# FFN's up product by Wo times W1 folded on the chip, W2's parts kept for two tiles, one gather per tile

## The chip, the cores and the metric

The kernel runs on one core of a Trainium2 chip. The metric is the device time of one execution in microseconds (us), as the median of the runs shown. The engines are TensorE (PE, with its weight loads shown apart as PEld), VectorE (DVE), ScalarE (ACT), GpSimd (POOL) and SyncE (SP, which here only issues DMAs).

## What is computed

The layer takes `x` of 2 x 1024 tokens with 256 channels. A mixture of experts, then attention, then a residual sum give `x2`. What the change touches comes behind that:

```python
def _L0_cond2_ref(x, ...):                 # a state space block, N = 64 states
    ...
    state = decay * state + dt * b_t * u_t # scan over the 1024 tokens
    ys = c_t * state                       # [B, L, 64]
    return y @ Wo + bo                     # Wo is [64, 256]; called x3 below

def _L0_ffn_ref(x3, Wr, br, W1, W2):       # 8 experts, each token uses one
    route = sigmoid(x3 @ Wr + br)
    max_prob, max_ind = max(route), argmax(route)
    out[token] = max_prob * (gelu(x3 @ W1[e]) @ W2[e])   # e = max_ind; W1 256x1024, W2 1024x256
x = x2 + _L0_ffn_ref(_L0_cond2_ref(x2, ...), ...)
```

## The kernel before

All matrix work that has to be precise is done with fp32r operands split in two: `hi` is the operand rounded to fp32r (a copy on ACT), `lo` is what is left (a subtraction on DVE), and a product is three matmuls, hi times hi, hi times lo and lo times hi (`three`, L1676).

The last part of the kernel has two stages. In the **routing stage** the 64 states of every token are in `seq_u` (one batch in each half of the partitions). PE makes the router's logits from them (`make_logits`), and DVE, ACT and PE find the expert of each token, its place among the tokens of that expert, and from that `token_s` (which token stands in which lane of which tile), `prob_s` and `tile_i` (the expert of each tile). Meanwhile PE makes x3 = y Wo + bo for all tokens (`bias_x3`, `make_x3`), ACT copies it out of PSUM (`x3_to_sbuf`) and stores it to the DRAM tensor `x3_d` (`store_x3`); SP has stored x2 to `x2_d`. Between these, `keep_warm` runs matmuls whose result nobody reads.

In the **tile stage** the tokens are worked on in 23 tiles of 128 tokens, each of one expert. For a tile POOL gathers its rows of x3 (`load_x3`) and of x2 (`load_x2`) with an indirect DMA each and scatters the result (a third one, L767). PE turns the tile's x3 (`turn_x`, 2 transposes), makes the up product (`half_up` twice, 12 matmuls of 512 columns: 2 chunks of 128 channels x 2 halves x 3), turns the hidden tile (`turn_h`, 8 transposes) and makes the down product (`expert_down`, 24 matmuls of 256 columns in two halves). ACT does gelu, the hi parts of x, W1, W2 and the hidden tile; DVE the lo parts of the same four and the final sum with x2 (`o_tile`). The weights of all experts are in SBUF as fp32 (`w_all`), and the expert of a tile is read into a register of ACT and DVE (`place_of_expert`), as the address of the weights to split. The split weights have one buffer (`w_hi`, `w_lo`), but for W1 of the second tile (`w1b_hi`, `w1b_lo`).

The order on each engine is written out by hand: on PE a tile is `turn_h(s)`, `expert_up(s + 1)`, `turn_x(s + 2)`, `expert_down(s)`. PE runs tiles 1 to 20 in a loop of two tiles; ACT and DVE have the first six steps and the last two written out. SP loads experts 0 to 3 behind the attention, and 4 to 7 once the first tiles' rows are gathered.

Of the kernel before, what the change touches and what calls it, by code (L numbers as in the profile page):

```python
# [27 lines left out]
P = 128  # L28
NB, L, C = 2, 1024, 256
CK = C // P  # L30
# [33 lines left out]
W1B_ROOM = 5  # L64
# [6 lines left out]
def layer_kernel(nc, a, out):  # L71

    with ExitStack() as ctx:
# [26 lines left out]
        w_hi = sb("w_hi", [P, 4, CK * 512], F32R, [split_at])  # L100
        w_lo = sb("w_lo", [P, 4, CK * 512], F32R, [split_at + 16384])
# [17 lines left out]
        bo_at = cursor[0]  # L119
        bo_wide = sb("bo_wide", [P, CK, P], F32)  # L120
        bo_high = sb("bo_high", [2, C], F32R, [bo_at])
        bo_part = sb("bo_part", [2, C], F32, [bo_at])
        bo_row = sb("bo_row", [2, C], F32)
        bo_split = sb("bo_split", [2, C], F32R)
        ones_r = sb("ones_r", [2, P], F32R)
# [90 lines left out]
        at = [x_at[1]]  # L216
        ctxT = [sb(f"ctxT_{i}", [P, 2, CK, P], F32, at) for i in range(2)]

        w_all = sb("w_all", [P, RE, CK * FF + FC * C], F32, [top])
        at = [stage]  # L220
        x2T = sb("x2T", [P, CK, T], F32, at)
        convT = sb("convT", [P, CK, T], F32, at)
        woT = sb("woT", [P, CK, P], F32, [at[0]])
        lane_hot = sb("lane_hot", [P, TT, P], F32R, at)
        tile_hot = sb("tile_hot", [P, TT, 3, TW], F32R, at)
        x3_tm = sb("x3_tm", [P, TT, C], F32, [stage + 16384])
# [22 lines left out]
        xs = [sb(f"xs_{i}", [P, C], F32, at) for i in range(2)]  # L249
        x2s = [sb(f"x2s_{i}", [P, C], F32, at) for i in range(2)]  # L250
        xsT_hi = [sb(f"xsT_hi{i}", [P, CK, P], F32R, at) for i in range(2)]
        xsT_lo = [sb(f"xsT_lo{i}", [P, CK, P], F32R, at) for i in range(2)]
        fh = [sb(f"fh_{i}", [P, FF], F32, at) for i in range(2)]
        fhT_hi = sb("fhT_hi", [P, FC, P], F32R, at)
        fhT_lo = sb("fhT_lo", [P, FC, P], F32R, at)
        fo = [sb(f"fo_{i}", [P, C], F32, at) for i in range(2)]
        assert at[0] <= top
        at = [top + (RE - 1 - W1B_ROOM) * WE]
        w1b_hi = sb("w1b_hi", [P, 2, CK * 512], F32R, at)
        w1b_lo = sb("w1b_lo", [P, 2, CK * 512], F32R, at)  # L260
        assert at[0] <= top + (RE - W1B_ROOM) * WE
# [18 lines left out]

        def x3_bank(w):
            return (0, 1, 2, 3, 4, 5, 0, 1)[w]


        parts_d = nc.dram_tensor("parts_d", [NB, 4, 2, P, L], F32).ap()
        x3_d = nc.dram_tensor("x3_d", [T, C], F32).ap()
# [1848 lines left out]
```

## Time and profile before

| | us |
|---|---|
| median of 3 runs (794.11, 794.45, 796.13) | 794.45 |
| span of the profiled execution, first to last instruction | 793.7 |
| attention ends, x2 and the states are made | about 552 to 597 |
| routing stage, until the first tile's rows are turned | 597 to 618 |
| tile stage, first gelu to last gelu | 625.1 to 776.1 |
| last gelu to the end | 17.6 |

Of the span PE is busy 97%, ACT 66%, DVE 60%, POOL 32%. These shares are means over stages with different limits: in the tile stage PE is busy 99%, DVE 94% and ACT 87% of the time; in the routing stage a chain of short DVE operations runs while PE is filled. A row of the timeline gives the start, how long it lasted, engine, line, operation, out<-in by the program's names, shapes, and in brackets how long the engine sat idle before it and what released it. A duration there is that of one instruction from start to end; instructions overlap by some, so the distance between two starts is what an engine needs for one more.

### The profile page before, as it was taken

To read this page: it belongs to the slowest core of one execution; us is meant where nothing else is said; L and a number is where in the kernel's file an instruction comes from. 1 tells how busy PE (TensorE), PEld (TensorE's weight loads), DVE (VectorE), ACT (ScalarE), POOL (GpSimd) and SP (SyncE) were. 2 spreads that over 40 slices of the span, in tenths; PEclk is the share of its full clock that TensorE was granted. 3 is DMA by queue.
4 is the path that set the end of the run, shared out by engine and by line. 5 is a ranking of instruction groups with operands and counts; after the bars stand their busy time and mean duration, and the time that the engine had idled before them with its cause. 6 is when DMAs were issued, how large, how long until landed. Compare 5 with 4: busy or idle time off the path is not lost.

```text
span 793.7 us, 13176 instructions
## 1 busy us (share of the span) xinstructions
PE 771.0 (97%) x4438; PEld 510.2 (64%) x4438; DVE 477.7 (60%) x859; ACT 521.8 (66%) x700; POOL 251.1 (32%) x310
## 2 busy tenths in 40 slices
PE   8999999999999999999999999999999899999994
PEld 5778888887777887533332332332655688888884
DVE  5887776639866763284331211211458699999994
ACT  4432222455233226799999999999466688888882
POOL 6444544314433421410000000100000477666652
PEclk9999999999999999999999999999999999999998
DMA  8241111101133704032752531500593681111000
GB/s 245 41 82 43 38 53 53 54 1 53 35 122 111 174 12 81 1 60 75 133 152 35 80 60 21 81 2 1 193 324 119 228 283 54 51 55 37 25 12 0
DMA packets 52762, 64.99 MB, mean 82 GB/s; under 512 B 15969, under 2 KB 44009, under 8 KB 52716
## 3 DMA queue, kind: packets, MB, share of 16 engines
q1 hardware_dynamic: 44580, 55.96, 27.5%
q0 software_dynamic: 3312, 6.31, 2.6%
q10 hardware_dynamic: 4824, 2.12, 1.0%
q8 instruction: 27, 0.44, 0.3%
q14 instruction: 19, 0.16, 0.1%
HBM read 51.52 MB, written 15.60 MB: 85 GB/s over the span
## 4 chain that ended last, share of the span: by engine, by line
PE 57%; ACT 20%; DVE 11%; issue 9%; DVEq 1%; DMA 1%; ACTq 1%; POOLq 0%; SPq 0%
PE psum L1676 40%; ACT pexp L848 15%; PE psum L1781 5%; PE psum L1768 4%; DVE w_lo L1546 3%; PE psum L1869 2%; ACT w_hi L1025 2%; PE psum L2060 2%; DVE hl L1084 1%; DVE hh L1232 1%; ACT w_hi L1030 1%; DVE ssum L1272 1%; DMA x_tm<-in_x 1%; DVEq L476 1%; DVE w_lo L1541 1%
## 5 line engine op out<-in xcount | busy, mean ns | idle before, releaser
L848 ACT ACTIVATE pexp<-psum 128x1024 f32<-128x1024 f32 x256 | 236.5, 1135 | 2.7 <-PE psum L1768 2.6
L835 ACT ACTIVATE hid<-psum,b_col 128x512 f32<-128x512 f32 x96 | 66.1, 688 | 163.1 <-PE psum L1676 123.1
L1781 PE MATMUL psum<-pexp,v_ones 128*32 128x512 f32 x1024 | 136.2, 605 | 0.4 <-ACT pexp L848 0.4
L1768 PEld LDWEIGHTS psum<-q_stack,k_stack 48*128 48x128 f32 x512 | 44.1, 184 | 114.6 <-ACT pexp L848 103.4
L1084 DVE SCALAR_TENSOR_TENSOR hl<-hid,scale_col,hh 128x341 fp32r<-128x341 f32 x192 | 104.7, 587 | 3.4
L1768 PE MATMUL psum<-q_stack,k_stack 48*128 48x512 f32 x512 | 106.2, 471 | 0.0
L1232 DVE TENSOR_SCALAR hh<-hid,scale_col 128x341 fp32r<-128x341 f32 x192 | 71.0, 411 | 57.5 <-ACT hid L835 40.2
L1358 DVE COPY yT<-psum 128x512 f32<-128x512 f32 x16 | 11.1, 691 | 122.8 <-PE psum L1781 122.8
L1676 PE MATMUL psum<-hh,w2h 128*128 128x512 f32 x192 | 76.6, 399 | 1.8 <-DVE hl L1084 1.7
L1676 PE MATMUL psum<-x_hi,w1h 128*128 128x512 f32 x192 | 77.0, 401 | 0.6 <-DVE x_lo L1098 0.6
L1676 PE MATMUL psum<-hh,w2l 128*128 128x512 f32 x192 | 75.0, 391 | 0.0
L1676 PE MATMUL psum<-x_hi,w1l 128*128 128x512 f32 x192 | 74.9, 390 | 0.0
L1676 PE MATMUL psum<-hl,w2h 128*128 128x512 f32 x192 | 74.9, 390 | 0.0
L1676 PE MATMUL psum<-x_lo,w1h 128*128 128x512 f32 x192 | 74.9, 390 | 0.0
L682 POOL CAST w1h<-raw 128x256 fp32r<-128x256 f32 x48 | 20.9, 436 | 155.9 <-PE psum L1676 144.2
L1676 PE MATMUL psum<-w_hi,fhT_hi 128*128 128x256 f32 x184 | 55.3, 301 | 3.5 <-DVE fhT_lo L1553 1.5
L1541 DVE TENSOR_TENSOR w_lo<-w_all,w_hi 128x1024 fp32r<-128x1024 f32 x44 | 51.9, 1222 | 9.4 <-ACT w_hi L1025 9.4
L1546 DVE TENSOR_TENSOR w_lo<-w_all,w_hi 128x1024 fp32r<-128x1024 f32 x46 | 55.9, 1216 | 1.6 <-ACT w_hi L1030 1.6
L710 POOL COPY v_ones<-v_tm 128x512 f32<-128x512 f32 x8 | 4.8, 612 | 161.1 <-PE psum L1781 161.1
L1676 PE MATMUL psum<-w_hi,fhT_lo 128*128 128x256 f32 x184 | 51.5, 280 | 0.0
L1676 PE MATMUL psum<-w_lo,fhT_hi 128*128 128x256 f32 x184 | 51.4, 279 | 0.0
L1030 ACT CAST w_hi<-w_all 128x1024 fp32r (+1 forms) x46 | 48.6, 1060 | 0.9 <-PE psum L1676 0.9
(286 smaller groups left out, 1436.3 us busy)
## 6 DMA issues: line engine op xcount, KB each, us to landing
w_all<-in_L_ffn_W SPq DMA_DIRECT2D x16, 1024.0 KB, 7.9
raw<-in_L_cond_ew SPq DMA_DIRECT2D x32, 256.0 KB, 3.2
parts_d<-parts SPq DMA_DIRECT2D x8, 1024.0 KB, 4.1
q_stack<-parts_d SPq DMA_DIRECT2D x48, 128.0 KB, 4.3
k_stack<-parts_d SPq DMA_DIRECT2D x48, 128.0 KB, 6.9
raw<-in_L_cond_sw SPq DMA_DIRECT2D x16, 256.0 KB, 3.7
x_tm<-in_x SPq DMA_DIRECT2D x4, 512.0 KB, 7.5
x_d<-x_tm SPq DMA_DIRECT2D x2, 1024.0 KB, 11.3
```

Source lines behind the costliest of these rows:

```text
L682: pool.tensor_copy(w1h[k][:], r1).then_inc(w_part, 1)
L835: act.activation(hid[k % 4][:], bank(k % 4), ACT.Gelu_apprx_tanh, bias=b1_col[:, bass.ds(4 * q + k // 2, 1)]).then_inc(gelu_done, 1)
L848: act.activation(pexp[mt % 2][:, 2 * j:2 * j + 2, 512 * h:512 * h + 512], psum[:, 2 * r:2 * r + 2, :], ACT.Exp, scale=D ** -0.5)\
L1025: act.copy(split_quarter(w1b_hi if isinstance(s, int) and s == 1 else w_hi, h), quarter(e, h))\
L1030: act.copy(split_quarter(w_hi, 2 + q), quarter(e, 2 + q)).then_inc(w2_hi, 1)
L1084: return dve.scalar_tensor_tensor(out=out, in0=in0, scalar=scalar, in1=in1, op0=op0, op1=op1)
L1232: ins = dve.tensor_scalar(hh[k % 4][:, x0:x1], hid[k % 4][:, x0:x1], w[r], None, ALU.mult)
L1541: dve.tensor_tensor(split_quarter(lo, h), quarter(e, h), split_quarter(hi, h).bitcast(F32), ALU.subtract).then_inc(w1_split, 1)
L1546: dve.tensor_tensor(split_quarter(w_lo, 2 + q), quarter(e, 2 + q), split_quarter(w_hi, 2 + q).bitcast(F32), ALU.subtract).then_inc(w2_spli ...
L1676: ins = pe.matmul(o, w[i], x[j], start=first and n == 0, stop=last and n == 2)
L1768: ins = pe.matmul(psum[:, 2 * r + lane, :], k_stack[i][rows, j, mt * P:(mt + 1) * P], q_stack[i][rows, j, 512 * h:512 * h + 512], start=Tr ...
L1781: ins = pe.matmul(psum[VW * j:VW * j + VW, 6 + h, :], v_ones[i][:, mt, j, :], pexp[mt % 2][:, j, 512 * h:512 * h + 512], start=(mt == 0), ...
```

## The change

The up product uses (y Wo + bo) W1 = y (Wo W1) + bo W1. Wo W1[e] (64 x 1024) and bo W1[e] are computed on the chip for each expert as plain fp32 matmuls (`fold`): four "bias" folds, each for two experts, and eight "fold" folds, in the order of `FOLDS`. Each fold goes through four engines: PE multiplies, ACT copies it out of PSUM (`copy_fold`), POOL splits it into fp32r hi and lo (`split_fold`, a copy and a subtraction of 128x512), SP moves the parts to their place in `t_all` (`move_fold`, 8 DMAs for a bias fold, 4 for the others). Eight folds are in the routing stage, and one in each of tiles 0 to 3. All four engines use two buffers for them, taken in turn.

The rows that a tile gathers are x2 and, next to it in the same DRAM tensor `rows_d`, the states y twice (384 values): one gather per tile, four tiles ahead, behind the first six folds in POOL's order. The x3 product, its copies, its stores and `keep_warm` go; ACT copies and stores the turned states instead (`copy_rows`, `store_rows`).

In a tile the up product is 4 matmuls of 512 columns (contraction 128: y's hi part on T's hi and lo parts, one above the other; contraction 66: y's lo part on T's hi part, and two rows of ones on the bias' parts). PE reads the tile's expert itself, as the address in `t_all`. W1 is no longer split; the parts of W2 have two buffers, and the sum of a tile goes to one of two PSUM banks. `turn_h` is two groups of 4 transposes, one behind each half of `down`. All engines have all tiles written out. W1 comes on SP as of the attention's seventh group; W2 of experts 1 to 7 is loaded between the moves.

```diff
+FOLDS = [("bias", 0), ("fold", 0), ("fold", 1), ("bias", 2), ("fold", 2), ("fold", 3),
+         ("bias", 4), ("fold", 4), ("fold", 5), ("bias", 6), ("fold", 6), ("fold", 7)]
+FIRST_FOLDS = 8
+XS = 4
...
@@ sync
+            def move_fold(k):
+                what, e = FOLDS[k]
+                sp.wait_ge(fold_split, k + 1)
+                if what == "bias" and e != 2:
+                    sp.wait_ge(folded, FOLDS.index(("fold", e + 1 if e else 0)) + 1)
+                high, low = fold_hi[k % 2], fold_lo[k % 2]
+                if what == "fold":
+                    for h in range(2):
+                        sp.dma_start(t_all[half[0], RE - 1 - e, :, h, :].bitcast(F32),
+                                     wide(high[half[h], :].bitcast(F32), 1, 2)).then_inc(fold_moved[k % 2], 16)
+                        sp.dma_start(t_all[half[1], RE - 1 - e, 0, h, :].bitcast(F32),
+                                     low[half[h], :].bitcast(F32)).then_inc(fold_moved[k % 2], 16)
+                else:
+                    for j in range(4):
+                        for row, part in ((N, high), (N + 1, low)):
+                            sp.dma_start(t_all[row:row + 1, RE - 1 - e - j // 2, 1, j % 2, :].bitcast(F32),
+                                         part[32 * j:32 * j + 1, :].bitcast(F32)).then_inc(fold_moved[k % 2], 16)
...
+            for k in range(FIRST_FOLDS - 2):
+                move_fold(k)
+                if k % 3 == 2:
+                    load_w2(k // 3 + 1)
+            sp.wait_ge(rows_stored, 16 * 2 * NB)
+            for i in range(XS):
                 sp.wait_ge(xs_in[i], 16)
+            load_w2(3)
+            for k in range(FIRST_FOLDS - 2, FIRST_FOLDS):
+                move_fold(k)
+            load_w2(4)
+            move_fold(FIRST_FOLDS)
+            load_w2(5)
+            load_w2(6)
+            for k in range(FIRST_FOLDS + 1, len(FOLDS)):
+                move_fold(k)
+            for k in range(len(FOLDS) - 2, len(FOLDS)):
+                sp.wait_ge(fold_moved[k % 2], moves(k))
+            load_w2(7)
...
@@ gpsimd
+            def split_fold(k):
+                i = k % 2
+                pool.wait_ge(fold_out, k + 1)
+                if k >= 2:
+                    pool.wait_ge(fold_moved[i], moves(k - 2))
+                pool.tensor_copy(fold_hi[i][:], fold_raw[i][:]).then_inc(fold_high, 1)
+                pool.wait_ge(fold_high, k + 1)
+                pool.tensor_tensor(fold_lo[i][:], fold_raw[i][:], fold_hi[i][:].bitcast(F32), ALU.subtract)\
+                    .then_inc(fold_split, 1)
...
+            for k in range(FIRST_FOLDS - 2):
+                split_fold(k)
+            pool.wait_ge(rows_base, 2 + XS)
             pool.wait_ge(tokens_known, 1)
             pool.wait_ge(x2_stored, 16 * NB)
+            pool.wait_ge(rows_stored, 16 * 2 * NB)
...
+            for s in range(XS):
+                load_rows(s)
+            for k in range(FIRST_FOLDS - 2, FIRST_FOLDS + 1):
+                split_fold(k)
             for s in range(TILES):
...
                 pool.wait_ge(fo_out, s + 1)
+                if s + XS < TILES:
+                    load_rows(s + XS)
                 pool.indirect_dma_start(out=out_rows,
...
+                if FIRST_FOLDS + 1 + s < len(FOLDS):
+                    split_fold(FIRST_FOLDS + 1 + s)
@@ scalar
+            def copy_fold(k):
+                act.wait_ge(folded, k + 1)
+                after(act, fold_split, k - 1)
+                act.copy(fold_raw[k % 2][:], bank(fold_bank(k))).then_inc(fold_out, 1)
...
+            copy_fold(0)
             act.activation(act_warm[:], ones[0:1, 0:1], ACT.Sigmoid)
+            copy_rows(0)
             act.wait_ge(logits_out, 1)
             act.activation(route[:], route[:], ACT.Sigmoid).then_inc(route_done, 1)
+            store_rows(0)
+            copy_rows(1)
+            store_rows(1)
+            for k in range(1, FIRST_FOLDS - 2):
+                copy_fold(k)
...
+            for s in range(TILES):
+                if s + 1 < TILES:
+                    place = place_of_expert(act, s + 1)
+                    gelu_tile(s + 1)
+                    w2_hi_part(s + 1, place, 0)
+                if s + 2 < TILES:
+                    x_hi_part(s + 2)
+                if s + 1 < TILES:
+                    h_hi_part(s + 1, 0)
+                if FIRST_FOLDS + s < len(FOLDS):
+                    copy_fold(FIRST_FOLDS + s)
+                if s + 1 < TILES:
+                    w2_hi_part(s + 1, place, 1)
+                    h_hi_part(s + 1, 1)
@@ vector
+            for s in range(TILES):
+                if s + 2 < TILES:
+                    x_lo_part(s + 2)
+                if s + 1 < TILES:
+                    place = place_of_expert(dve, s + 1)
+                    w2_lo_part(s + 1, place, 0)
+                    h_lo_part(s + 1, 0)
+                dve.wait_ge(xs_in[s % XS], 16 * (s // XS + 1))
+                o_tile(s)
+                if s + 1 < TILES:
+                    w2_lo_part(s + 1, place, 1)
+                    h_lo_part(s + 1, 1)
@@ tensor
+            def fold(k):
+
+                what, e = FOLDS[k]
...
+                elif 3 <= k < FIRST_FOLDS:
+                    pe.wait_ge(fold_out, k - 2)
...
+                for c in range(CK):
+                    if what == "bias":
+                        for j in range(4):
+                            ins = pe.matmul(psum[32 * j:32 * j + 32, fold_bank(k), :], bo_wide[:, c, 0:32],
+                                            w1_raw[e + j // 2][:, c, 512 * (j % 2):512 * (j % 2) + 512],
+                                            start=(c == 0), stop=(c == CK - 1))
+                    else:
+                        for h in range(2):
+                            ins = pe.matmul(psum[half[h], fold_bank(k), :], woT[:, c, half[h]],
+                                            w1_raw[e][:, c, 512 * h:512 * h + 512],
+                                            start=(c == 0), stop=(c == CK - 1))
...
+            fold(0)
             make_logits(0)
+            turn_rows(0)
+            fold(1)
             make_logits(1)
+            turn_rows(1)
+            fold(2)
...
             rank()
+            for k in range(3, 6):
+                fold(k)
...
+            for k in range(6, FIRST_FOLDS):
+                fold(k)
...
+                for h in range(2):
+                    pe.matmul(psum[:, 2 * i + h, :], yy_hi[i][:],
+                              t_all[:, bass.ds(place, 1), 0, h, :].rearrange("p e n -> p (e n)"),
+                              start=True, stop=False)
+                    ins = pe.matmul(psum[:, 2 * i + h, :], y1_lo[i][0:N + 2, :],
+                                    t_all[0:N + 2, bass.ds(place, 1), 1, h, :].rearrange("p e n -> p (e n)"),
+                                    start=False, stop=True)
...
+            for s in range(TILES):
+                if s + 2 < TILES:
+                    place = place_of_expert(pe, s + 2)
+                down(s, 0)
+                if s + 2 < TILES:
+                    turn_x(s + 2)
+                if FIRST_FOLDS + s < len(FOLDS):
+                    fold(FIRST_FOLDS + s)
+                if s + 1 < TILES:
+                    turn_h(s + 1, 0)
+                down(s, 1)
+                if s + 1 < TILES:
+                    turn_h(s + 1, 1)
+                if s + 2 < TILES:
+                    up(s + 2, place)
```

## Rows read from the trace of the kernel before

**Rows 1.** Stages of PE: busy time, granted clock, DMA share, GB/s.

```profile
620.00:624.00 4.00, 3.76 (x11) 0.57 0.46 150
628.00:776.00 148.00, 146.59 (x970) 1.00 0.26 84
```

**Rows 2.** Timeline of ACT: first gelu, one tile's work, last gelu.

```profile
625.12 1.03 ACT L1014 ACTIVATE fh<-psum 128x1024 f32<-128x1024 f32 x1 [1.22 <-PE psum L1676]
...
649.57 1.03 ACT L1014 ACTIVATE fh<-psum 128x1024 f32<-128x1024 f32 x1 [0.69 <-PE psum L1676]
650.49 0.37 ACT L1053 CAST xsT_hi<-psum 128x256 fp32r<-128x256 f32 x1
...
652.64 1.05 ACT L1030 CAST w_hi<-w_all 128x1024 fp32r x1
...
776.12 1.02 ACT L1014 ACTIVATE fh<-psum 128x1024 f32<-128x1024 f32 x1 [0.73 <-PE psum L1676]
```

**Rows 3.** Timeline of PE over one tile.

```profile
645.75 1.03 PE L2060 MATMUL psum<-ident,fh 128*128 128x128 f32 x8
646.53 0.48 PE L1676 MATMUL psum<-w_hi,xsT_hi 128*128 128x512 f32 x1
...
649.37 0.38 PE L2036 MATMUL psum<-ident,xs 128*128 128x128 f32 x2
...
649.98 0.28 PE L1676 MATMUL psum<-w_lo,fhT_hi 128*128 128x256 f32 x1
...
651.15 0.28 PE L1676 MATMUL psum<-w_hi,fhT_lo 128*128 128x256 f32 x1
```

**Rows 4.** Timeline of DVE over one tile, and its last sum.

```profile
654.62 1.22 DVE L1546 TENSOR_TENSOR w_lo<-w_all,w_hi 128x1024 fp32r<-128x1024 f32 x1
655.75 1.28 DVE L1553 TENSOR_TENSOR fhT_lo<-psum,fhT_hi 128x512 fp32r<-128x512 f32 x2
...
658.23 0.42 DVE L1559 TENSOR_TENSOR xsT_lo<-psum,xsT_hi 128x256 fp32r<-128x256 f32 x1
...
785.46 0.48 DVE L1084 SCALAR_TENSOR_TENSOR fo<-psum,prob_s,x2s 128x256 f32<-128x256 f32 x1 [1.39 <-PE psum L1676]
```

**Rows 5.** Reads of `tile_i` into a register of DVE: ns min/median/max, first and last start.

```profile
L476 DVEq TENSOR_LOAD <-tile_i x44: 297/306/555, 619.8 to 775.6; - x44
```

**Rows 6.** Timeline of PE: four fp32 matmuls 128x64 by 512 columns each.

```profile
586.22 1.94 PE L1950 MATMUL psum<-convT,wp_sb 128*64 128x512 f32 x8 [0.27 <-issue]
587.96 1.92 PE L1950 MATMUL psum<-x2T,ws_sb 128*64 128x512 f32 x8
```

**Rows 7.** Timeline of PE: four fp32 matmuls 128x32 by 512 columns, attention.

```profile
461.79 1.07 PE L1781 MATMUL psum<-pexp,v_ones 128*32 128x512 f32 x8
```

**Rows 8.** POOL's splits and gathers: ns min/median/max, first and last start.

```profile
L682 POOL CAST w1h<-raw x48: 395/398/756, 6.3 to 285.4; 128x256 fp32r<-128x256 f32 x48
L684 POOL TENSOR_TENSOR w1l<-raw,w1h x48: 722/738/925, 6.8 to 285.9; 128x256 fp32r<-128x256 f32 x48
L744 POOL DMA_INDIRECT x2s<-x_d,token_s x23: 998/2039/2047, 618.3 to 776.8; - x23
```

**Rows 9.** Timeline of SP: one small DMA, six stack DMAs.

```profile
26.45 0.60 SPq L543 DMA_DIRECT2D bp_c<-in_L_cond_bp  x1
498.40 2.63 SPq L590 DMA_DIRECT2D q_stack<-parts_d  x6
```

**Rows 10.** DMA issues: queue, operation, KB each, median us from issue to landing.

```profile
w_all<-in_L_ffn_W SPq DMA_DIRECT2D x16, 1024.0 KB, 7.9
...
x_d<-x_tm ACTq DMA_DIRECT2D x8, 256.0 KB, 2.4
```

**Rows 11.** Timeline: the first two gathers, the first turn of a tile's rows.

```profile
615.02 1.24 POOL L744 DMA_INDIRECT xs<-x_d,token_s  x1 [2.80 <-DMA x_d<-x_tm]
616.58 1.44 POOL L744 DMA_INDIRECT xs<-x_d,token_s  x1 [0.31 <-issue]
...
618.08 0.44 PE L2036 MATMUL psum<-ident,xs 128*128 128x128 f32 x2 [0.70 <-DMA xs<-x_d,token_s]
```

More of the change, by code:

```diff
@@ L415, in layer_kernel @@
         rows_base = sem("rows_base")
-        x2s_in = [sem(f"x2s_in{i}") for i in range(2)]
         out_stored = [sem(f"out_stored{i}") for i in range(2)]
@@ new lines, in copy_rows, with store_rows @@
+            def copy_rows(n):
+                act.wait_ge(rows_turned, n + 1)
+                by_tile = rows_bank(n).rearrange("p (i b n) -> p b i n", b=NB, n=N)
+                for d in range(2):
+                    for b in range(NB):
+                        act.copy(y_rows[:, b, 4 * n:4 * n + 4, d, :], by_tile[:, b]).then_inc(rows_out, 1)
+            def store_rows(n):
+                act.wait_ge(rows_out, 4 * n + 4)
+                for b in range(NB):
+                    act.dma_start(y_rows_d[n, b][:, :, C:], y_rows[:, b, 4 * n:4 * n + 4, :, :].rearrange(
+                        "p i d n -> p i (d n)")).then_inc(rows_stored, 16)
@@ L1928, in _ @@
             project(7)
-            def keep_warm(n, cols=512):
-                for k in range(n):
-                    pe.matmul(bank(6)[:, 0:cols], ident[:], projT[:].rearrange("p k c -> p (k c)")[:, 0:cols],
-                              start=(k == 0), stop=(k == n - 1))
             def sequence(k, n):
@@ L2048, in expert_up, with turn_x, up @@
-            def expert_up(s, i):
+            for k in range(6, FIRST_FOLDS):
+                fold(k)
+            def turn_x(s):
+                pe.wait_ge(xs_in[s % XS], 16 * (s // XS + 1))
+                after(pe, x_lo_out, s - 1)
+                after(pe, fo_out, s - 2)
+                pe.transpose(turned_row(s), xs[s % XS][:, C:], ident[:]).then_inc(xs_turned, 1)
+            def up(s, place):
+                if s < RE:
+                    for k, (what, e) in enumerate(FOLDS):
+                        if (what == "fold" and e == s) or (what == "bias" and e == s - s % 2):
+                            pe.wait_ge(fold_moved[k % 2], moves(k))
@@ L2099, in _, with down @@
-            expert_down(0, 0)
-            with pe.Fori(0, (TILES - 3) // 2) as m:
-                tile(2 * m + 1, 1, m + 2)
-                tile(2 * m + 2, 0, m + 3)
-            turn_h(TILES - 2, 1)
-            expert_up(TILES - 1, 0)
-            expert_down(TILES - 2, 1, between=lambda: turn_h(TILES - 1, 0))
-            expert_down(TILES - 1, 0)
+            def down(s, q):
+                if q == 0:
+                    after(pe, fo_out, s - 1)
+                pe.wait_ge(fhT_lo_out, 2 * s + q + 1)
+                pe.wait_ge(w2_split, 2 * s + q + 1)
+                for f in range(4 * q, 4 * q + 4):
+                    w = slice((f % 4) * C, (f % 4 + 1) * C)
+                    ins = three(out_bank(s), (fhT_hi[:, f, :], fhT_lo[:, f, :]),
+                                (w2_part(w_hi, s, q)[:, w], w2_part(w_lo, s, q)[:, w]), f == 0, f == FC - 1)
+                ins.then_inc(w2_used, 1)
@@ new lines, in _ @@
+            pe.wait_ge(slots_done, 1)
+            turn_x(0)
+            turn_x(1)
+            up(0, RE - 1)
+            up(1, place_of_expert(pe, 1))
+            for h in range(2):
+                turn_h(0, h)
+            for s in range(TILES):
[13 more added lines that the diff above has]
+                    up(s + 2, place)
```

450 lines of the change are left out of this document (147 added, 303 removed).

## The prediction

> **What bounds the kernel now.** I read the stages first. In the tile stage, 148 us long, PE is busy 99% of the time at the full clock, 2.4 GHz [rows 1]; before it there are some us at a mean of 0.57, near the lower level of 1.2 GHz. The gelus mark the rounds: the first starts at 625.12, the 23rd at 776.12 [rows 2], so 22 steps take 151.0 us. Next the timeline of one tile. PE: 8 transposes from 645.75 to 646.53, that is 0.78; 12 up matmuls from 646.53 to 649.37, 2.84 or 0.23 each; 10 steps of the down product from 649.98 to 651.15, 0.117 each [rows 3]. So a tile is 0.8 + 2.8 + 24 x 0.117 = 2.8 + 0.25 for turning x, 6.7 us of PE, against 151.0 / 22 = 6.9 per step. DVE has as much: four splits of weights at 1.13 (from one start to the next), two of the hidden tile at 0.6, 0.42 for x and 0.4 to 0.5 for the sum [rows 4], 6.6. ACT: gelu 0.92, x 0.25, four casts at 0.95, two at 0.5, 6.0 [rows 2]. The three stand close together, PE in front. So a change that relieves PE alone would gain little; this one takes from all three.
>
> **A round, afterwards.** PE loses 8 of 12 up matmuls (8 x 0.23 = 1.85) and one turn: 4 x 0.23 + 0.8 + 2.8 + 0.1 = 4.65. DVE loses two splits of weights (2.26) and half of x: 4.2. ACT loses two casts (1.9): 4.0. No engine is the bound alone, so I follow the longest chain that closes on itself: from a gelu to the gelu two tiles on. Gelu 0.92, W2's cast 0.95, x's cast and the hand-over 0.35, x's subtraction and then, on DVE, the read of the expert, which nothing covers there: 0.70 (the read alone 0.31 [rows 5], the rest address steps, an estimate), W2's split 1.13, hidden 0.60, sum 0.40, W2's split 1.13, hidden 0.68 and a hand-over 0.16, 12 down matmuls 1.41, 4 transposes 0.47, 4 up matmuls 1.12. Sum 10.0 for two tiles, 5.0 a round. Bounds: 4.65, where PE's work alone counts, and 5.4, where PE's own read of the expert, of which the trace has no row, comes on top of that work with all of 0.7. I take 5.0, since PE then has 0.35 to spare and DVE's row is the nearest. The first step (two ups back to back) stays short, 2.9. So 2.9 + 21 x 5.0 = 107.9 instead of 151.0: **-43.1** (-50 to -35).
>
> **The folds on PE.** A fold is four fp32 matmuls 128x64 by 512, exactly what the rows at 586.22 and 587.96 show: 1.74 from one start to the next [rows 6]. A bias fold is eight of 128x32; four of these side by side took about 1.0 in the attention [rows 7], so 2.0. The eight in the routing stage lie beside DVE's chain: the second logits wait for two of them, some 0.8 us, and the placing matmuls for three more, 1.3 in all; the next paragraph covers both. Four are in tiles 0 to 3, and PE works through them: 3 x 1.74 + 2.0 = **+7.2** (5 to 9).
>
> **The start.** Here the change adds a chain, and POOL's order puts the gathers behind it. Before, the first gather went out at 615.02 and its rows were turned at 618.08; the second gather came 1.56 later [rows 11]. Now six `split_fold` come first. One costs POOL a cast and a subtraction of 128x512; the rows have 0.40 and 0.74 for half the width [rows 8], so about 0.7 + 1.3 + hand-overs = 2.1. From the third on a split waits until the fold two before it has been moved. A move of a plain fold is 4 issues at 2.63 / 6 = 0.44 on SP [rows 9], then 768 KB; 256 KB landed in 2.4 us [rows 10], so I take 3.7, 5.5 together. A bias fold is 8 issues of one 2 KB row each, 0.55 (0.44 to 0.60, [rows 9]), 4.4, and 2.4 to land. ACT copies fold 1 only behind the sigmoid's table, the copies of the rows and their four stores, at about 607.6. So: split 1 until 609.7; split 2 until 612; move 1 lands at 609.7 + 5.5 = 615.2, split 3 until 617.3; split 4 (move 2 lands at 617.6) until 619.8; move 3, of a bias, 617.3 + 4.4 + 2.4 = 624.1; split 5 until 626.2. Only then the first gather goes out, 11 us later than before. Rows turned at 629.3, the second tile's at 630.9; both ups stand behind both turns, x's two steps and the first up at the low clock (PE has waited for the gather, as it had before the stretch at 0.57 [rows 1]) take 2: first gelu at about 632.8, where it was at 625.1: **+7.7**. Bounds: -3, if the moves are fast enough that the tokens gate the gathers as before (the splits of W1 between 618 and 625 are gone), and +12, if the moves queue on the DMA rings behind the 1 MB of W2, which took 7.9 to land [rows 10].
>
> **Waits in the first tiles.** The same chain goes on. POOL holds the gather for tile 4 behind `split_fold(8)`, that behind fold 8 in tile 0 and the landing of move 6, which SP issues only when fold 8 is done: 4.4 + 2.4 behind it, and a W2 load before it. By the rounds above the rows of tile 4 come about 3 us late. ACT's `copy_fold(10)` waits for the same split, and the next up for that copy. The gather of tile 7 and W2 of expert 7 stand likewise behind `split_fold(11)` and the last moves: another 3, and W2 some 1.5. **+7.5** (0 to 14: nothing where the moves take half, twice as much where bulk loads hold them up). From tile 9 on POOL has one gather (2.0) and one scatter (1.2) in 5 us, and nothing is late.
>
> **The tail.** From the last gelu to the end were 17.6 us; the second W2 buffer lets the last split start before the tile before is through, about **-1.3** (-2 to 0). The scatters and what follows stay. W1's loads in the attention fall into a time with little DMA, and x2's store has less in front of it: nothing.
>
> **The sum.** 7.7 - 43.1 + 7.2 + 7.5 - 1.3 = -22.0. The span of the profiled execution is 793.7, and the median of the runs 794.45, 0.75 above; with that around it, 793.7 - 22.0 + 0.75 = 772.4 us.
>
> **A rule against it.** The rows show POOL's cast of W1 between 395 and 756 ns for one shape, and the gather between 998 and 2047 [rows 8], while DVE's split of W2 keeps its 1.22 [rows 4]. The Trainium skill, "SBUF — State Buffer", section "SBUF: two separate sides", says that a DVE instruction with two SBUF inputs and a GpSimd one that reads SBUF exclude each other for the whole instruction, whichever starts first. By that, a gather could hold DVE's split of W2 for 1.0 us in a round. Here the rows have the gather wait and not the split, so I leave it out of the sum; it is the third rival.
>
> **Rivals.** *The folds' chain does not gate* (0.15): the gathers go out with the tokens and nothing is late in tiles 4 to 8: 772.4 - 10.7 - 7.5 = 754, and 754 to 764 where half of it stays. For it: 2 KB rows inside SBUF may land sooner than any row here. Against: the issues alone are 4.4 and 1.8 of SP each. *The chain is longer* (0.2): each move 1.5 us more and W2 in front: +4 at the start, +6 in the tiles, 780 to 786. *POOL's work holds DVE* (0.07): a gather and a scatter each put about 0.8 us into the chain of a round: 21 x 0.8 = 17, 789. *The other side* (0.06): PE's read of the expert stands right before the down product, each round. If PE's sequencer takes longer for it than the others, or runs dry behind it, the round is 4.65 + that cost; it exceeds 5.0 from 0.35 on, and the kernel is slower from 4.65 + 1.4 = 6.05. At 1.6 it is 772.4 + 21 x 1.25 = 799. For it: PE had no such read before. Against: the read takes 0.31 on DVE, and PE has other work queued. *The change doesn't do what it says* (0.02), rounds near 6.9 still: then 772.4 + 40 = 812.
>
> **How the numbers follow.** The forecast, 766 to 780, has 0.5. The range leaves out the lower half of the first rival, the last two and some of the third: 760 to 785. A difference of 0.3%, 2.4 us, is about what a measurement of this kernel can tell from none. Faster 0.91; within 0.3%: 0.03, the edge between the third and the fourth rival; slower 0.06.
>
> **What would show it.** Right: gelus about 5.0 us apart from tile 9 on, PE busy below 95% of such a round; the first gather at 623 to 629, right behind the sixth split on POOL; single steps of 7 to 9 us among the first eight, that end with a gather, a move or a W2 load. Wrong: gelus 5.5 or more apart; a first gather near 615; PE idle behind its own read; W2's splits on DVE longer than 1.3; the fp32 folds at other than 1.74.

## The result and the profile after

| | before | after |
|---|---|---|
| median of five runs, us | 794.45 (794.11 to 796.13) | 787.46 (785.82 to 792.27) |
| profiled execution: time, span, us | span 793.7 | 786.71, span 784.9 |
| first gelu, last gelu, us | 625.12, 776.12 | 637.72, 770.69 |
| last gelu to the end of the span, us | 17.6 | 14.2 |

The ratio of the times is 0.9913, with a 95% interval of 0.9891 to 0.9934: faster, but by 7 us and not by the 22 of the forecast (772.4, range 760 to 785). Timeline of ACT in the changed kernel, the gelus that start a tile's work (start, duration, engine and line, output and input, idle time before and what ended it); they answer to [rows 2]:

```profile
637.72 1.02 ACT L1049 ACTIVATE fh<-psum 128x1024 f32<-128x1024 f32 x1 [1.51 <-PE psum L2056]
...
655.25 1.03 ACT L1049 ACTIVATE fh<-psum 128x1024 f32<-128x1024 f32 x1 [0.27 <-PE psum L2056]
670.51 1.03 ACT L1049 ACTIVATE fh<-psum 128x1024 f32<-128x1024 f32 x1 [0.28 <-PE psum L2056]
677.27 1.03 ACT L1049 ACTIVATE fh<-psum 128x1024 f32<-128x1024 f32 x1 [0.27 <-PE psum L2056]
687.84 1.02 ACT L1049 ACTIVATE fh<-psum 128x1024 f32<-128x1024 f32 x1 [6.05 <-PE psum L2056]
...
699.32 1.04 ACT L1049 ACTIVATE fh<-psum 128x1024 f32<-128x1024 f32 x1
...
770.69 1.03 ACT L1049 ACTIVATE fh<-psum 128x1024 f32<-128x1024 f32 x1 [0.35 <-PE psum L2056]
```

From the ninth gelu (699.32) to the 23rd are 14 steps of 5.10, as forecast. The loss is ahead of them: the first gelu is 12.6 later than before (forecast 7.7), and the first eight steps take 61.6 (forecast 52.6), with one of 15.3 and one of 10.6 among them. The stages of PE (stretch, its length, busy time, granted clock, DMA share, GB/s) show both long steps as an idle stretch, full of DMA, and 4 us at 0.50 of full speed, the lower level of 1.2 GHz, behind it:

```profile
656.50:663.00 6.50, 0.27 (x3) 0.78 1.01 289
663.00:667.00 4.00, 3.99 (x9) 0.50 1.08 307
667.00:681.00 14.00, 14.00 (x104) 1.00 0.36 109
681.00:686.00 5.00, 0.44 (x3) 0.81 0.95 220
686.00:690.00 4.00, 4.00 (x16) 0.50 0.93 236
...
699.00:771.00 72.00, 70.54 (x524) 1.00 0.13 41
```

What held PE, by its own timeline, that of POOL, that of SP (the first and the last issue of move 6, of a bias fold, and the first of move 9) and that of ACT (the copy of fold 8):

```profile
663.01 0.47 PE L2040 MATMUL psum<-ident,xs 128*128 128x128 f32 x1 [6.25 <-DMA xs<-rows_d,token_s]
663.42 3.68 PE L1996 MATMUL psum<-w_raw,woT 128*64 128x512 f32 x8
...
671.93 1.94 PE L1996 MATMUL psum<-w_raw,woT 128*64 128x512 f32 x8
...
685.74 0.79 PE L2053 MATMUL psum<-t_all,yy_hi 128*128 x1 [4.56 <-issue]
```

```profile
627.78 1.24 POOL L781 DMA_INDIRECT xs<-rows_d,token_s  x1 [0.16 <-issue]
...
651.35 0.61 POOL L761 CAST fold_hi<-fold_raw 128x512 fp32r<-128x512 f32 x1 [13.47 <-DMA t_all<-fold_lo]
652.04 2.18 POOL L763 TENSOR_TENSOR fold_lo<-fold_raw,fold_hi 128x512 fp32r<-128x512 f32 x1
654.37 1.03 POOL L781 DMA_INDIRECT xs<-rows_d,token_s  x1
```

```profile
645.18 0.56 SPq L638 DMA_DIRECT2D t_all<-fold_hi  x1
...
649.58 0.58 SPq L638 DMA_DIRECT2D t_all<-fold_lo  x1
...
673.96 0.56 SPq L638 DMA_DIRECT2D t_all<-fold_hi  x1
```

```profile
646.20 0.59 ACT L1019 COPY fold_raw<-psum 128x512 f32<-128x512 f32 x1
```

Folds, splits, moves and tiles are counted from 0, as in the code. The long step starts at SP: it begins move 6 when fold 8 is done, and the eight issues take 5.0. POOL has stood 13.47 at the split of fold 8, with the gather for tile 4 behind it. Up to 646.8 it would have stood in any case, since ACT's copy of fold 8 ends there; the last 4.6 are for move 6. The gather goes out at 654.37 and its rows are turned at 663.01, 8.6 later, where the first gather of before needed 3.1 [rows 11]. PE stands 6.25, and the next fold runs at half clock, 3.68 where 1.9 is usual. The step of 10.6 is the other end of the chain: the first up of tile 6 waits 4.6. The profile names no releaser for it; by the code it waits for moves 9 and 10, and SP may start move 9 only behind fold 11 (671.93 on PE, 673.96 on SP).

### The profile page after: what moved, and what is told of

Read it like the earlier page. It is cut to its first block and busy times, and to the rows that moved or that the text cites. A ratio compares the mean times of both kernels' runs of the same rounds, so it can differ in the third digit from the quotient of the medians.

```text
span 784.9 us, 12562 instructions
## 1 busy us (share of the span) xinstructions
PE 744.9 (95%) x4313; PEld 478.2 (61%) x4313; DVE 430.2 (55%) x812; ACT 481.9 (61%) x665; POOL 217.7 (28%) x309
## 5 line engine op out<-in xcount | busy, mean ns | idle before, releaser
L1555 DVE TENSOR_TENSOR w_lo<-w_all,w_hi 128x1024 fp32r<-128x1024 f32 x46 | 58.0, 1263 | 11.6 <-issue 10.6
L1686 PE MATMUL psum<-w_hi,fhT_hi 128*128 128x256 f32 x184 | 55.2, 300 | 3.0 <-DVE fhT_lo L1561 2.5
L1686 PEld LDWEIGHTS psum<-hh,w2h 128*128 128x128 f32 x192 | 36.0, 188 | 12.2 <-DVE hl L1110 4.4
```

The lines of the kernel that those rows point to most:

```text
L1555: dve.tensor_tensor(w2_part(w_lo, s, q), w2_quarter(place, q), w2_part(w_hi, s, q).bitcast(F32), ALU.subtract).then_inc(w2_split, 1)
L1686: ins = pe.matmul(o, w[i], x[j], start=first and n == 0, stop=last and n == 2)
```

## Experiments

Theory A: POOL's order and the two buffers of the folds tie gathers, splits and moves into one chain, and that chain is the loss. Theory B: the bulk loads of W2 on the same DMA rings are. Theory C: PE's own folds and the low clock are. All figures of gelus are from the profiled execution of each run, totals are medians; 787.5 is the changed kernel. A gelu given by its number counts from 0, as the tiles do (the step from gelu 3 to 4 is the fourth step); one given by its rank (the ninth gelu) counts from the first. The changed kernel was not run again beside the experiments. The kernel before was, with medians of 794.8 to 795.6 instead of 794.45, so a difference to 787.5 is good to about 1 us; where that matters the ratio to before stands with it (0.9913 for the changed kernel).

**Without the last four folds.** Their copies, splits and moves are out too, move 6 no longer waits for fold 8, and tiles of experts 5 to 7 use expert 4's weights.

```
-         ("bias", 4), ("fold", 4), ("fold", 5), ("bias", 6), ("fold", 6), ("fold", 7)]
+         ("bias", 4), ("fold", 4)]
```

> Left out: the last four folds (W1 of expert 5, the biases of experts 6 and 7, W1 of experts 6 and 7) with their copies, splits and moves; tiles of these experts use expert 4's weights. Theory A (their chain makes the waits of the first tiles): the eight steps from the first gelu to the ninth fall from 61.6 to 39 to 43, total 766 to 769. Theory C (PE's work on these folds is the cost): they fall by 7 to 8 only, to 54, total 779. Theory B (bulk loads of W2, which here come in one burst): they fall by PE's 7 and the waits stay, total 778 to 782.

Measured: 765.3; first gelu 637.46, the first eight steps 41.4. As A had it, or a little below. Three of the eight steps still hold a wait of PE for rows, 0.92, 0.73 and 0.90, beside the burst of W2.

**PE's late folds alone.** As in that run, but PE still does four folds.

```
+LATE_FOLDS = [("fold", 6), ("bias", 6), ("fold", 6), ("fold", 7)]
```

> As the run without the last four folds, but PE still works through four folds (16 + 4 fp32 matmuls) in tiles 0 to 3; left out are only their copies, splits and moves. So the difference to that run is PE's share, and the difference to the changed kernel is the chain's. Theory A: 4 x 1.8 to 2.0 = 7.2 to 8 us above the run without them, 774 to 776, and 11 to 13 below the changed kernel. Theory C: at or near the changed kernel, 784 to 787. Below 7 above the other run, 767 to 772: PE's folds fill gaps that are there anyway.

Measured: 771.25, the first eight steps 47.6. That is the third of the forecasts: PE's share is 6.2 in the profile (6.0 in the medians), below 7.2, though the four folds take 7.5 by PE's timeline, so some of them lies in gaps that are there anyway. And the rest of the chain costs 61.6 - 47.6 = 14.0 (16.2 in the medians). That is the term the forecast had at 7.5.

**Thin loads of W2.** 128 KB each for experts 1 to 7; every tile uses expert 0's W2.

```
+                f = FC if e == 0 else 1
-            return w2_all[:, bass.ds(place, 1), 1024 * q:1024 * q + 1024].rearrange("p e n -> p (e n)")
+            return w2_all[:, RE - 1, 1024 * q:1024 * q + 1024]
```

> Left out: seven eighths of the loads of W2 of experts 1 to 7 (the loads stand where they did, with 128 KB each instead of 1 MB); all tiles use expert 0's W2, whose load is whole. Theory B (bulk loads on the DMA rings hold rows and moves back): gathers land 3 us after their issue instead of 5 to 9, the steps from gelu 0 to 8 fall from 61.6 to about 48 and the first gelu from 637.7 to about 633; total 769 to 772. Theory A (order and waits of the folds' chain): the first gelu 2 to 3 sooner, the step 3 to 4 about 5 shorter since its rows land sooner, the step 5 to 6 as it was: total 778 to 781. If the issues on SP alone count: 785 to 787.

Measured: 782.5, between A and B. The gather for tile 4 now lands 5.2 after its issue instead of 8.6, and the step falls from 15.3 to 11.8; the next long one stays at 10.2, the first gelu at 637.26. But not all of the 5.0 is B's. The last 14 steps, behind W2's loads, are 4.95 instead of 5.10, which is 2.1 of it: W2 is read at a fixed place here, and DVE stands 0.36 instead of 0.47 ahead of a tile's first split. First a row of the changed kernel, then one of this run:

```profile
738.41 1.23 DVE L1555 TENSOR_TENSOR w_lo<-w_all,w_hi 128x1024 fp32r<-128x1024 f32 x1 [0.47 <-issue]
```

```profile
739.25 1.23 DVE L1556 TENSOR_TENSOR w_lo<-w_all,w_hi 128x1024 fp32r<-128x1024 f32 x1 [0.36 <-issue]
```

The first eight steps fall by 2.0 only, from 61.6 to 59.6, since the first two are 2.0 longer here (the cause is open), and the first gelu comes 0.5 sooner. So B has about 2.5, with 3.5 in that one landing. A's forecast of 2 to 3 at the start was wrong: the loads of W2 do not delay the first gathers; what else lies on the rings there, the moves, was not taken away.

**The gather of tile 4 ahead of the split.**

```
-            for k in range(FIRST_FOLDS - 2, FIRST_FOLDS + 1):
+            for k in range(FIRST_FOLDS - 2, FIRST_FOLDS):
                 split_fold(k)
...
+                if s == 0:
+                    split_fold(FIRST_FOLDS)
```

> Only POOL's order is changed: the gather for tile 4 and the first scatter stand ahead of the split of fold 8 instead of behind it. Theory A (the folds' chain holds the rows back through POOL's order): the gather goes out with the first sum, near 649 instead of 654.4, the step from gelu 3 to gelu 4 falls from 15.3 to 8 to 10, the step from gelu 5 to 6 stays near 10 since the moves of folds 9 and 10 come no sooner; total 780 to 782 (787.5 before the edit). Theory B (the bulk loads of W2 on the same DMA rings hold the rows back): the gather goes out sooner but lands 8 us later all the same beside W2 of experts 3 and 4; the step stays above 12, total 784 to 786. Theory C (PE's own fold work and the low clock it leaves behind): no change, 786 to 788.

Measured: 784.2, 3.3 less (ratio to before 0.9854, 0.9836 to 0.9872). The total is B's, but the steps are not: the one is 7.2, shorter than even A had it, and the next is 14.6. Timeline of POOL and PE in this run:

```profile
649.98 1.48 POOL L781 DMA_INDIRECT xs<-rows_d,token_s  x1 [12.75 <-DVE fo L1112]
...
660.09 1.29 POOL L761 CAST fold_hi<-fold_raw 128x512 fp32r<-128x512 f32 x1 [4.12 <-DMA t_all<-fold_lo]
...
662.93 1.06 POOL L781 DMA_INDIRECT xs<-rows_d,token_s  x1
```

```profile
670.38 0.48 PE L2042 MATMUL psum<-ident,xs 128*128 128x128 f32 x1 [5.15 <-DMA xs<-rows_d,token_s]
```

The wait has only moved on by a tile: now the gather of tile 5 stands behind the split of fold 9, and that one waits for move 7. The profiled execution took 787.15, the longest of the four, and its first eight steps add up to 62.6, no less than the 61.6 of the changed kernel; so these steps do not show where the 3.3 come from.

**All gathers of the first tiles ahead of splits.** The split of fold 8 is out of the loop ahead of the tiles, as in the run before.

```
-                if FIRST_FOLDS + 1 + s < len(FOLDS):
-                    split_fold(FIRST_FOLDS + 1 + s)
+                if FIRST_FOLDS + s < len(FOLDS):
+                    split_fold(FIRST_FOLDS + s)
```

> POOL's order again, now for all of the first four tiles: each tile's gather and scatter go out ahead of the split of one fold (fold 8 after the first, 9 after the second, 10, 11). Theory A: the step of 14.6 from gelu 4 to 5 that the first reordering left (its gather stood behind the split of fold 9) falls to 7 or 8, steps 3 to 4 near 7.2, the step 5 to 6 stays at 9 to 10.6 for the moves of folds 9 and 10: total 777 to 779. Rival (the wait only travels on to the next tile again, since POOL's work is late in all): total 783 to 785.

Measured: 782.7 (ratio to before 0.9845, 0.9822 to 0.9868). The steps are as A had them, 7.2, 7.5 and 10.2, the first eight 55.2; but the median lies 4 us above A's range, near the rival's 783, and the profiled execution, the shortest of the four, took 781.26. One later step, from the ninth gelu to the tenth, is 7.5 here instead of 6.1. ACT's cast of W2 for tile 7 stood 2.0 for the load of expert 7, which SP issues behind the last moves. PE then waits for DVE twice, 1.0 each, and its granted clock is below full from 692 to 700 (stages of PE as above):

```profile
689.46 1.04 ACT L1056 CAST w_hi<-w_all 128x1024 fp32r x1 [2.00 <-DMA w_all<-in_L_ffn_W]
```

```profile
692.00:696.00 4.00, 2.95 (x16) 0.75 0.02 6
696.00:700.00 4.00, 4.00 (x27) 0.83 0.20 65
```

**Three buffers.** The folds' fp32r parts get a third buffer, so a split waits for the move three folds before it. It lies where constants are no longer needed; nothing else is changed. (PE has three PSUM banks for the first eight folds already in the changed kernel; the two buffers are ACT's copies and POOL's parts, and only the parts get a third.)

```
-                i = k % 2
+                i, r = k % 3, k % 2
...
-                if k >= 2:
-                    pool.wait_ge(fold_moved[i], moves(k - 2))
+                if k >= 3:
+                    pool.wait_ge(fold_moved[i], moves(k - 3))
```

> Three buffers instead of two for the folds' fp32r parts: a split waits for the move three folds before it. Theory A (splits stand behind moves, gathers behind splits): the sixth split ends near 622 instead of 627.6, the first gather goes out near 623 and the first gelu starts near 633 to 634; the split of fold 8 no longer waits for move 6, the gather for tile 4 goes out near 649 instead of 654.4, so the step from gelu 3 to 4 falls from 15.3 to 8 to 10; the step 5 to 6 stays near 10 (the moves of folds 9 and 10 still wait for fold 11). Total 775 to 779. Theory B (the DMA rings are what is slow, whatever the order): the gathers go out sooner but land beside the moves and W2 loads that they now meet, total 783 to 786.

Measured: 774.1, 13.3 less than the changed kernel. First gelu 632.78 (-4.9), the first eight steps 55.2 (-6.4). Waits of POOL between 600 and 700 us (what waited and for what: total, times, longest), first of the changed kernel, then of this one, and the timeline of this one's POOL at the gathers of tiles 0 and 4:

```profile
POOL fold_hi L761 <- DMA t_all<-fold_lo: 29.4, 6, 13.5
```

```profile
POOL fold_hi L765 <- DMA t_all<-fold_lo: 2.9, 2, 2.0
```

```profile
622.94 1.24 POOL L785 DMA_INDIRECT xs<-rows_d,token_s  x1 [0.18 <-issue]
...
643.48 1.85 POOL L785 DMA_INDIRECT xs<-rows_d,token_s  x1
```

The splits' 29.4 us of waiting for moves shrink to 2.9, and the first gather goes out 4.8 sooner, that of tile 4 10.9 sooner. The step from gelu 3 to 4 is 7.2, below A's 8 to 10, the step from 5 to 6 stays at 11.0, as A had it, and the total is 1 below A's range. Of the 15 us by which the forecast was missed this one edit gives 13 back: A, and more exactly the second buffer that a move must leave first.

**Three edits together:** three buffers, gathers first, and a bias fold moved by 4 DMAs of two rows.

```
-                    for j in range(4):
+                    for j in range(2):
...
-                                         part[32 * j:32 * j + 1, :].bitcast(F32)).then_inc(fold_moved[k % 2], 16)
+                                         part[64 * j + 31:64 * j + 33, :].bitcast(F32))\
+                                .then_inc(fold_moved[k % 3], 16)
```

> Three edits together: three buffers, every gather ahead of the splits of its tile, and a bias fold moved by 4 DMAs of 2 rows instead of 8 of one (SP then needs 2.5 us instead of 5.0 for it). Theory A: start as with three buffers or 1 us sooner (first gelu near 633), no wait for rows in tiles 4 and 5, the step 5 to 6 down by some 2.5 to 8: total 770 to 775. Theory B: the DMA rings hold, 778 to 783.

Measured: 773.4, as A had it, but within 1 us of three buffers alone. Once hardly a split waits for a move, POOL's order and SP's issues together are worth next to nothing. The steps from gelu 4 on move both ways (9.1, 11.0 and 6.0 become 7.9, 8.1 and 8.0), so one of the two may give what the other takes; they were not taken apart.

**PE filled in its long wait.** Six idle products of 512 columns ahead of the turn of tile 4.

```
+                for n in range(6 if s == 2 else 0):
+                    pe.matmul(bank(4), ident[:], w1_raw[7][:, n % 2, 0:512], start=True, stop=True)
```

> The changed kernel, with PE kept at work in its longest wait: in the third tile, ahead of the turn that waits 6.25 us for the rows of tile 4, six idle fp32 products of 512 columns (about 5.3 us, into a PSUM bank that is free there). Theory (part of each wait's price is the low clock behind it): the fold behind it takes 1.9 instead of 3.68 and the turns and first products run at the full clock; the step from gelu 3 to 4 falls from 15.3 to about 13.2, total 785 to 786. Rival (the low clock costs nothing, since DVE and ACT are late there as well): step and total as they were, 787 to 788; or the products run past the landing and it is slower.

Measured: 785.55, the step 13.4, as forecast. PE's timeline, beside 663.01 and 663.42 above:

```profile
662.72 0.33 PE L2040 MATMUL psum<-ident,xs 128*128 128x128 f32 x1 [0.86 <-DMA xs<-rows_d,token_s]
662.97 1.94 PE L1996 MATMUL psum<-w_raw,woT 128*64 128x512 f32 x8
```

So 1.9 us of that step were the low clock behind the wait: the fold alone is 1.74 shorter. C has this part, by the timeline; the total alone doesn't show it, since its ratio to before, 0.9885 (0.9868 to 0.9901), and that of the changed kernel, 0.9913 (0.9891 to 0.9934), overlap.

**W2's parts for one tile only.**

```
-            return w[:, 2 * (s % 2) + q, :]
+            return w[:, q, :]
-                after(act, w2_used, 2 * s - 3 + q)
+                after(act, w2_used, 2 * s - 1 + q)
```

> One part undone: W2's fp32r parts are kept for one tile only, so ACT's cast of the next tile's first half waits for the down product of the same half. Theory of the rounds (the chain through ACT and DVE stands 0.35 behind PE): from the end of the first half of a down product cast 1.0, x's cast and subtraction 0.6, address read 0.5, split 1.15, hidden 0.7, hand-over 0.2 = 4.2 to 4.3, while PE has 3.6 of other work there: 0.6 to 0.7 a round, rounds of tiles 9 to 23 from 5.1 to 5.7 or 5.8, total 797 to 802 (787.5 before the edit). Rival (rounds are PE's work alone and the second buffer hides nothing): within 1 of 787.5.

Measured: 797.6, and the last 14 steps 5.72 each. That is the 0.6 more in each round that the expectation had for the chain through the single buffer, and the second buffer alone is worth 10 us. It shows that this chain bounds the round without the second buffer; it does not show what bounds it with two.

**Towards a faster kernel.** Two more on top of the three edits: PE filled ahead of the placing products, then the gathers of tiles 0 and 1 ahead of the sixth split (with it, PE waits ahead of the second turn until ACT has copied the sixth fold).

```
+            for n in range(WARM):
+                pe.matmul(bank(4), ident[:], w1_raw[3][:, n % 2, 0:512], start=True, stop=True)
             pe.wait_ge(token_hot, 1)
```

> The version with three edits, and PE filled with four idle fp32 products of 512 columns (about 3.5 us, into a PSUM bank nobody reads) in the 3.2 us in which it waits for the one-hot rows at 615 to 618. Theory (low clock is part of the price: PE's placing products took 3.59 and 3.61 and the next fold 3.20 there, where they take 1.9 to 2.0 at the full clock, and the first turn follows directly behind them): first gelu 3 to 4 sooner, as long as the gathers (issued at 623.5, landing 5.6 to 6.7 later) allow it, so 1 to 3: total 770.5 to 772.5. Rival (the gathers' landing ends last): within 0.7 of 773.4.

> As the run with the filled PE, and the gathers of tiles 0 and 1 stand ahead of the split of the sixth fold on POOL (those of tiles 2 and 3 behind it). Theory A (gathers wait for splits): first gather about 621 instead of 623.5, first gelu 2 sooner than in the run before: 768 to 771. Rival (the tokens or the landing end last): within 1 of that run.

Measured: 775.1 and 772.6. The first was a miss, 1.7 above the version it starts from: the filled PE did the first placing products in 2.19 instead of 3.59, then waited 1.36 for DVE, and the next ones took 3.61 again:

```profile
617.89 2.19 PE L2033 MATMUL psum<-tile_hot,lane_hot 128*128 128x24 f32 x16
621.44 3.61 PE L2038 MATMUL psum<-tile_hot,lane_hot 128*128 128x48 f32 x16 [1.36 <-DVE tile_hot L1542]
```

The two folds behind them took 3.64 and 3.02, where the version with three edits had 3.20 and 1.94, and the first gelu came 1.35 later. The second has a median 2.5 lower than the first, but its total is above A's 768 to 771: its first gather goes out at 622.41, behind the making of `token_s`, not at 621, and its first gelu is 1.3 sooner, not 2. The ratios of the two overlap (0.9724 to 0.9757 and 0.9696 to 0.9750), and neither is clear of the version with three edits (0.9699 to 0.9732).

Last, two folds in each of tiles 0 and 1. ACT's copies and POOL's splits follow (that of fold 8 stands ahead of the first tile's gather again), and W2 of expert 6 is loaded behind the moves instead of ahead of them:

```
+                if s < 2:
+                    fold(FIRST_FOLDS + 2 * s)
                 if s + 1 < TILES:
                     turn_h(s + 1, 0)
+                if s < 2:
+                    fold(FIRST_FOLDS + 2 * s + 1)
```

> As the run before, and the four late folds are done two a tile in tiles 0 and 1 instead of one a tile in 0 to 3, so that the bias move of experts 6 and 7, which waits for the last fold, starts near 650 instead of 661. Theory A: the waits at tile 6 (2.8 of PE's idle time and 2 to 3 of low clock behind it) go, 4 to 6 sooner than the run before: 763 to 767. Theory B (the moves then meet W2's loads on the DMA rings and land no sooner, or ACT stands behind the splits): within 2 of the run before or slower.

Measured: 770.4 (ratio to before 0.9681, 0.9652 to 0.9710), the lowest median of those that do the whole work and better than both kernels, but 2.2 less than the run before it instead of 4 to 6, and not clear of it (0.9696 to 0.9750). The long steps have changed place: 11.4 between the second gelu and the third, 9.2 between the sixth and the seventh. Whether the moves could be kept out of the way wholly was not tried; 765.3, without these folds, is 5 below.

## Why the prediction was wrong

The span was to fall from 793.7 to 771.7 and is 784.9, 13.2 above. The median lies another 1.8 above, since it stands 2.6 over that span and 0.75 was added: 0.75 was the median of the runs less the span of one execution, while every execution with both on record takes 1.8 to 1.9 more than its own span; by that, the one profiled before lay about 1 above its median. By the terms of the sum:

| term | forecast | measured | from |
|---|---|---|---|
| start | +7.7 | +12.6 | first gelus |
| 22 steps without late folds and their chain | -43.1 | -38.2 | 41.4 + 71.4 against 151.0 |
| folds on PE | +7.2 | +6.2 | PE's folds alone |
| waits in the first tiles | +7.5 | +14.0 | 61.6 - 47.6 |
| tail | -1.3 | -3.4 | 17.6 to 14.2 |

**Rounds: right in the main.** 5.10 from the ninth gelu on (forecast 5.0). The term is 4.9 short because the first eight steps without the late folds take 41.4 instead of 37.9, 3.5 of it, and 14 times 0.1 the rest; of the 3.5, 2.6 are the three waits for rows beside W2's loads. One sign failed: PE was to be busy below 95% of a round, and is for 70.5 of 72 us. Its own work is nearer 4.8 than 4.65 (the first up of a tile takes 0.32 and the first product of a half 0.22), and the busy share counts a product to its modelled end (0.28, where the next starts 0.12 later), so that short gaps don't show in it. Still PE stands behind DVE in places:

```profile
744.70 0.68 DVE L1561 TENSOR_TENSOR fhT_lo<-psum,fhT_hi 128x512 fp32r<-128x512 f32 x1
```

```profile
745.07 0.39 PE L2056 MATMUL psum<-t_all,y_lo 66*128 x1
745.49 0.36 PE L1686 MATMUL psum<-w_hi,fhT_hi 128*128 128x256 f32 x1
```

The up at 745.07 would be done by 745.30; the down product starts at 745.49, behind DVE's subtraction. That the rounds with thin loads, where DVE's gap ahead of the split is 0.11 shorter, take 4.95 fits a chain through DVE, as the forecast had it; that run changes ACT's address too, so it doesn't settle it. No wait for PE's read of the expert is to be seen, so the fourth rival falls.

**Folds and tail.** A fold takes 1.87 from its start to the next and not 1.74, a bias fold 1.85 and not 2.0; with the gaps they fill, 6.2 in all. The tail is 3.4 shorter instead of 1.3, past its bound of 2. With one buffer for W2's parts it is 15.5 and not 14.2, so the second buffer gives just the 1.3; the other 2.1 are open.

**The start: mechanism right, size wrong.** The sixth split was to end at 626.2 and ended at 627.6. The first gather follows right behind, as forecast. But its rows were turned 5.3 after the issue, not 3.1, and those of the second at 635.43 instead of 630.9. POOL's splits 3 to 5, which wait for moves 1 to 3, and PE's first two turns:

```profile
616.20 0.73 POOL L761 CAST fold_hi<-fold_raw 128x512 fp32r<-128x512 f32 x1 [3.10 <-DMA t_all<-fold_lo]
...
619.45 0.61 POOL L761 CAST fold_hi<-fold_raw 128x512 fp32r<-128x512 f32 x1 [0.95 <-DMA t_all<-fold_lo]
...
625.63 0.61 POOL L761 CAST fold_hi<-fold_raw 128x512 fp32r<-128x512 f32 x1 [4.16 <-DMA t_all<-fold_lo]
626.32 1.30 POOL L763 TENSOR_TENSOR fold_lo<-fold_raw,fold_hi 128x512 fp32r<-128x512 f32 x1
```

```profile
633.12 0.44 PE L2040 MATMUL psum<-ident,xs 128*128 128x128 f32 x1 [5.10 <-DMA xs<-rows_d,token_s]
635.43 0.47 PE L2040 MATMUL psum<-ident,xs 128*128 128x128 f32 x1 [1.86 <-DMA xs<-rows_d,token_s]
```

The step that failed took the landing from a stretch where no moves were on the rings. The stages of PE (columns as above), first of before, then of after, have a DMA share of 0.15 there and of 0.98 here:

```profile
615.00:618.00 3.00, 2.39 (x10) 1.00 0.15 44
```

```profile
627.50:633.00 5.50, 0.52 (x4) 0.99 0.98 246
```

With thin loads of W2 the first landing is 5.1, so W2 is not what lengthens it; what does was not singled out. 12.6 is just past the bound of 12.

**Waits in the first tiles: the step that failed.** It has the right places, the gather of tile 4 behind `split_fold(8)` behind move 6. It sized the lateness of these rows as 3 and it was 6.25. It does not work the 3 out; the only landing of a gather that it has is the start's 3.1, and this one took 8.6 (5.2 with thin loads). It has no term for the low clock behind each wait (1.9 in this one); and the wait of tile 6 for moves 9 and 10, 4.6 long with half clock behind it, is missing from it. In its place it had 3 for the gather of tile 7, which PE did not wait for, and 1.5 for W2 of expert 7, for which ACT waited 1.27. The single steps were to be 7 to 9; the long ones are 15.3 and 10.6. Its upper bound, 14, was the value, but it was set for bulk loads that hold up the moves.

**The rivals.** The second, the longer chain, comes nearest; it was given 0.2 and 780 to 786. Its sizes, 4 at the start and 6 in the tiles, are about what came (4.9 and 6.5), but not by its mechanism: it had each move 1.5 longer, and from the end of their splits moves 1 to 3 took 5.8, 6.4 and 7.1 where the forecast had 5.5, 5.6 and 6.8, so 0.3 to 0.8 longer. The gathers' landings and the waits they cause are the larger part. The third, POOL's work beside DVE, is not the cause: W2's splits on DVE keep a median of 1.22 over the tiles.

The range did leave room for both late terms: at their bounds of 12 and 14 the sum is 783.2, inside 785. What takes the time to 787.5 is the 0.6 past the bound of the start, the 4.9 in the steps and the 1.8 from the span, less 3.1 in folds and tail.

## What to carry over

A chain with two buffers that ends in a DMA turns every slow transfer into a stop for whatever its engine does next; before ordering work around such a stop, ask what a third buffer costs, here 4 KB a partition for 13 us. When a gather is moved, take its landing from a stretch with the same traffic, not from a quiet one, and add what PE loses behind each wait. And compare like with like: the span of one execution with its own time, not with the median of others.

## What the hardware showed

Eight small DMAs in a row take longer to issue than one takes to land: a 2 KB row costs SP 0.63 from one issue to the next, so a bias fold of 16 KB holds SP for 5.0, while one such row lands in 1.9 to 2.3 (medians). The Trainium skill, "DMA: Bandwidth & Descriptors", section "Issuing engines are not separate DMA queues", calls the time to initiate a DMA usually small relative to the DMA itself; here one issue is about 0.3 of one row's landing, and eight of them exceed it. That fewer issues make this kernel faster is not shown: half of a bias fold's went in the run with three edits, which stayed within 1 us of the one with three buffers alone.

POOL's split and DVE's split of W2 lengthen each other: POOL's subtraction takes 2.18 instead of 1.3 at 652.04 (above), behind DVE's at 651.42, and one of DVE's takes 1.98 instead of 1.22 behind POOL's at 669.56:

```profile
669.56 1.31 POOL L763 TENSOR_TENSOR fold_lo<-fold_raw,fold_hi 128x512 fp32r<-128x512 f32 x1
```

```profile
651.42 1.62 DVE L1555 TENSOR_TENSOR w_lo<-w_all,w_hi 128x1024 fp32r<-128x1024 f32 x1 [0.48 <-issue]
...
669.97 1.98 DVE L1555 TENSOR_TENSOR w_lo<-w_all,w_hi 128x1024 fp32r<-128x1024 f32 x1
```

That bears out the rule on the shared port in the Trainium skill, "SBUF — State Buffer", section "SBUF: two separate sides": whichever starts first keeps the other off. It happens to three of DVE's splits, all in the first tiles; from 700 to 760, where POOL only gathers and scatters, their mean is 1.22.
